# Softmax attention: a quarter of the denominator summed by ScalarE beside the maxima, the rest by GpSimd in three groups

## The reference, cut to what matters

```python
xn = layer_norm(x, norm_w, norm_b)
q = (xn @ q_w + q_b).reshape(Bx, Tx, H, -1)
k = (xn @ k_w + k_b).reshape(Bx, Tx, H, -1)
att = jnp.einsum('bnhl,bmhl->bnmh', q, k)
att = att + (1.0 - mask) * -1000000.0
att = jax.nn.softmax(att, axis=2)
v = ((xn @ v_w + v_b) * src_mask[:, :, None]).reshape(Bx, Tx, H, -1)
y = jnp.einsum('bnmh,bmhl->bnhl', att, v).reshape(Bx, Tx, Dx)
```

## Time and profile before

| | before |
|---|---|
| median of 3 runs | 5798.27 us (5793.98 to 5799.08) |
| profiled execution: time, span | 5799.68 us, 5797.9 us |
| share of the span busy: PE, DVE, ACT, POOL | 91%, 71%, 49%, 57% |
| attention stage, first max matmul to last output | 2527.5 to 4354.4 us of the span |
| one head in the middle of it | 55.57 us |

### The profile page before, as it was taken

How to read it: one execution, slowest core, us unless ns; L and a number is a source line. 1 busy time by engine, 2 the same in 40 slices (tenths; PEclk the granted TensorE clock), 3 DMA queues, 4 the chain that set the end, 5 groups by cost and what they waited for, 6 DMA issues and landing times. The chain is left out here.

```text
span 5797.9 us, 58781 instructions
## 1 busy us (share of the span) xinstructions
PE 5261.4 (91%) x19584; PEld 2493.5 (43%) x19584; DVE 4122.4 (71%) x5430; ACT 2814.3 (49%) x4847; POOL 3282.8 (57%) x2136
## 2 busy tenths in 40 slices
PE   7888988888898869989999999999998889979998
PEld 2333333333333324444554554555444454544545
DVE  6999999999999963267777777777744445444454
ACT  3757566675756523326666666666661131312112
POOL 3879797887979741128888888888890000000000
PEclk9999999999999999979999999999998999989999
DMA  4021211212122023321111111111103201021101
GB/s 167 22 102 60 86 73 51 79 46 102 37 100 83 29 104 123 124 62 34 23 34 30 27 34 23 34 33 24 34 1 134 82 26 69 17 104 35 60 26 51
DMA packets 117503, 346.28 MB, mean 60 GB/s; under 512 B 13040, under 2 KB 14288, under 8 KB 102800
## 3 DMA queue, kind: packets, MB, share of 16 engines
q1 hardware_dynamic: 99280, 294.47, 15.4%
q0 software_dynamic: 9216, 33.56, 1.5%
q10 hardware_dynamic: 8704, 14.50, 0.7%
HBM read 274.29 MB, written 67.67 MB: 59 GB/s over the span
## 5 line engine op out<-in xcount | busy, mean ns | idle before, releaser
L1397 DVE TENSOR_REDUCE attn_mx<-attn_ps_max 128x1 f32<-128x512 f32 x2048 | 1270.3, 683 | 404.1 <-PE attn_ps_max L1268 399.6
L425 POOL TENSOR_TENSOR mamba_hc<-mamba_h,mamba_bc 128x1024 f32<-128x1024 f32 x512 | 1219.1, 2381 | 360.0 <-DVE mamba_h L658 306.4
L1363 ACT ACTIVATE attn_prob<-attn_ps_s 128x512 f32<-128x512 f32 x2048 | 1061.0, 603 | 589.9 <-PE attn_ps_s L1293 586.6
L805 PE MATMUL mamba_y<-mamba_hc,ident 128*128 128x512 f32 x2048 | 997.7, 610 | 272.2 <-POOL mamba_hc L425 269.9
L1251 POOL TENSOR_TENSOR attn_pair_sum<-attn_prob 128x1024 f32<-128x1024 f32 x384 | 907.6, 2386 | 311.0 <-ACT attn_prob L1363 310.9
L528 ACT ACTIVATE mamba_da<-mamba_dt,mamba_a_neg 128x512 f32<-128x512 f32 x1024 | 691.0, 689 | 722.0 <-DVE mamba_h L658 718.3
L658 DVE TENSOR_TENSOR_SCAN mamba_h<-mamba_da,mamba_state,mamba_h 128x512 f32<-128x512 f32 x768 | 939.8, 1265 | 1.9 <-ACT mamba_da L528 1.9
L1293 PE MATMUL attn_ps_s<-attn_q_stack,attn_k_stack 100*128 100x512 f32 x2048 | 861.6, 424 | 4.2 <-ACT attn_prob L1363 4.2
L1268 PE MATMUL attn_ps_max<-attn_k_stack,attn_q_stack 98*128 98x512 f32 x2048 | 835.7, 415 | 16.8 <-DMA attn_q_stack<-qk_parts 16.0
L805 PEld LDWEIGHTS mamba_y<-mamba_hc,ident 128*128 128x128 f32 x2048 | 366.3, 191 | 856.5 <-POOL mamba_hc L425 459.2
L648 DVE TENSOR_TENSOR mamba_h<-mamba_du,mamba_bc 128x1024 f32<-128x1024 f32 x512 | 619.3, 1210 | 65.5 <-POOL mamba_state L427 57.1
(11 more groups left out here) (232 smaller groups left out, 6076.5 us busy)
## 6 DMA issues: line engine op xcount, KB each, us to landing
mamba_bc<-bc_dram SPq DMA_DIRECT2D x64, 1024.0 KB, 7.3
mamba_w<-in_in_proj_w_T SPq DMA_DIRECT2D x16, 2048.0 KB, 7.8
qk_parts<-qkv_pair POOLq DMA_DIRECT2D x64, 512.0 KB
attn_k_stack<-qk_parts SPq DMA_DIRECT2D x96, 256.0 KB
attn_q_stack<-qk_parts SPq DMA_DIRECT2D x96, 256.0 KB
mamba_x_in<-in_x SPq DMA_DIRECT2D x16, 1024.0 KB, 5.3
mamba_w<-in_out_proj_w_T SPq DMA_DIRECT2D x8, 2048.0 KB, 8.3
lin_norm_x<-x_after_L SPq DMA_DIRECT2D x16, 1024.0 KB, 5.7
```

The source lines that it names most:

```text
L425: nc.gpsimd.tensor_tensor(hc[:, gs % HC_SLOTS, :, :], h[:, gs % H_SLOTS, :, :], bc[:, g, G:2 * G, :], ALU.mult).then_inc(s["hc_done"], 1)
L805: mm = nc.tensor.matmul(y[ct % 2][:, :], ident[:, :], hc[:, gs % HC_SLOTS, j, :], start=(g == 0 and j == 0), stop=(g == NG - 1 and j == G ...
L1363: nc.scalar.activation(prob[kt % SLOTS][:, c * CH:(c + 1) * CH], ps_s[n % BANKS][:, :], ACT.Exp).then_inc(s["exp_done"], 1)
L1397: nc.vector.tensor_reduce(mx[hd % 3][:, qt, kc:kc + 1], ps_max[seq % BANKS][:, :], AX.X, ALU.max).then_inc(s["bank_read"], 1)
```

## The change

Every fourth key tile (`u % 4 == 3`, 3, 7, 11 and 15) leaves GpSimd's sums. The key block of a max matmul is no longer 512 neighbouring keys but four runs of 128 with a step of 512, so that the fourth block of a query tile holds the keys of just these four tiles. VectorE's reduce writes the negated maximum of this block, and ScalarE reads the block's scores from the same bank with this as bias, takes the exponentials and lets the engine accumulate them along the row (`sum_own`, 16 per head, into `own_sum`). The difference between the block's own maximum and the query's maximum is made by VectorE, its exponential by ScalarE (`exp_gap`), and the product is the block's share of the denominator (`scale_own`). `read_o` adds it before the reciprocal. GpSimd sums the other twelve tiles in three groups of four (0, 1, 2, 4; 5, 6, 8, 9; 10, 12, 13, 14): 18 adds, three waves of ones. `TURN_O` and `DEN_LAG` go from 2 to 3.

```diff
-        SIZES = (2, 3, 3, 2, 3, 3)
-        GROUPS = [tuple(range(sum(SIZES[:g]), sum(SIZES[:g + 1]))) for g in range(len(SIZES))]
-        NGRP = len(GROUPS)
+        OWN = QB - 1
+        SUMMED = [u for u in range(QT) if u % QB != OWN]
+        NGRP = 3
+        GROUPS = [tuple(SUMMED[g * len(SUMMED) // NGRP:(g + 1) * len(SUMMED) // NGRP]) for g in range(NGRP)]
...
-        TURN_O = 2
-        DEN_LAG = 2
+        TURN_O = 3
+        DEN_LAG = 3
...
             def free_bank(seq):
                 if seq >= BANKS:
                     pe.wait_ge(s["bank_read"], seq - BANKS + 1)
+                    if SEQ_OWN[seq - BANKS]:
+                        pe.wait_ge(s["own_summed"], OWN_BY[seq - BANKS + 1])
                 return ps_max[seq % BANKS]
...
-                nc.tensor.matmul(free_bank(seq)[:, :], q_st[slot][0:ROWS_MAX, qt * P:(qt + 1) * P],
-                                 k_st[slot][0:ROWS_MAX, kc * CH:(kc + 1) * CH], start=True, stop=True).then_inc(s["bank_filled"], 1)
+                nc.tensor.matmul(free_bank(seq)[:, :].rearrange("p (a j) -> p a j", j=P), q_st[slot][0:ROWS_MAX, qt * P:(qt + 1) * P],
+                                 k_st[slot][0:ROWS_MAX, :].rearrange("r (a b j) -> r b a j", b=QB, j=P)[:, kc],
+                                 start=True, stop=True).then_inc(s["bank_filled"], 1)
...
+            def sum_own(seq, hd, i):
+
+                act.wait_ge(s["bank_read"], seq + 1)
+                nc.scalar.activation(own_exp[:, :], ps_max[seq % BANKS][:, :], ACT.Exp, bias=mx[hd % 3][:, i // QB, OWN:QB],
+                                     accum_out=own_sum[hd % 3][:, i // QB:i // QB + 1]).then_inc(s["own_summed"], 1)
+
+            def exp_gap(hd):
+                act.wait_ge(s["gap_made"], hd + 1)
+                nc.scalar.activation(own_gap[:, :], own_gap[:, :], ACT.Exp, scale=-1.0).then_inc(s["gap_exp"], 1)
+
+            for i in range(OWN, NMAX, QB):
+                sum_own(i, 0, i)
             first_part(NMAX, 0)
+            exp_gap(0)
+            for i in range(OWN, LEAD * PER, QB):
+                sum_own(NMAX + 1 + i, 1, i)
...
                         elif hd + 1 < HEADS:
                             exp(hd + 1, 0, c)
+                    for j, tile in enumerate(max_tiles(hd, u)):
+                        if own_block(tile[1]):
+                            sum_own(item_at(hd, "max", u, j), *tile)
                     if u == TURN_O - 1 and hd:
                         copy_den(hd - 1)
                     if u == TURN_MAX and hd + 1 < HEADS:
                         first_part(item_at(hd, "turn_max", u), hd + 1)
+                        exp_gap(hd + 1)
                 copy_o(hd)
...
-                nc.vector.tensor_reduce(mx[hd % 3][:, qt, kc:kc + 1], ps_max[seq % BANKS][:, :], AX.X, ALU.max).then_inc(s["bank_read"], 1)
+                nc.vector.tensor_reduce(mx[hd % 3][:, qt, kc:kc + 1], ps_max[seq % BANKS][:, :], AX.X, ALU.max,
+                                        negate=own_block(i)).then_inc(s["bank_read"], 1)
                 if i == NMAX - 1:
                     dve.wait_ge(s["bank_read"], seq + 1)
-                    nc.vector.tensor_reduce(m_all[:, :], mx[hd % 3][:, :, :], AX.X, ALU.max).then_inc(s["m_done"], 1)
+                    nc.vector.tensor_reduce(m_all[:, :], mx[hd % 3][:, :, 0:OWN], AX.X, ALU.max).then_inc(s["m_others"], 1)
+                    dve.wait_ge(s["m_others"], hd + 1)
+                    nc.vector.scalar_tensor_tensor(out=m_all[:, :], in0=mx[hd % 3][:, :, OWN], scalar=-1.0, in1=m_all[:, :],
+                                                   op0=ALU.mult, op1=ALU.max).then_inc(s["m_done"], 1)
+                    dve.wait_ge(s["m_done"], hd + 1)
+                    nc.vector.tensor_tensor(own_gap[:, :], mx[hd % 3][:, :, OWN], m_all[:, :], ALU.add).then_inc(s["gap_made"], 1)
+
+            def scale_own(hd):
+                dve.wait_ge(s["gap_exp"], hd + 1)
+                dve.wait_ge(s["own_summed"], (hd + 1) * QT)
+                nc.vector.tensor_tensor(own_den[hd % 2][:, :], own_sum[hd % 3][:, :], own_gap[:, :], ALU.mult).then_inc(s["own_scaled"], 1)
...
-                nc.vector.reciprocal(rden[:, :].rearrange("p (t c) -> p t c", c=QB),
-                                     ps_d[:, :].rearrange("p (t c e) -> p t c e", c=QB, e=DH1)[:, :, :, 0]).then_inc(s["den_inv"], 1)
+                dve.wait_ge(s["own_scaled"], hd + 1)
+                nc.vector.tensor_tensor(rden[:, :].rearrange("p (t c) -> p t c", c=QB),
+                                        ps_d[:, :].rearrange("p (t c e) -> p t c e", c=QB, e=DH1)[:, :, :, 0],
+                                        own_den[hd % 2][:, :].rearrange("p (c t) -> p t c", c=QB), ALU.add).then_inc(s["den_whole"], 1)
+                dve.wait_ge(s["den_whole"], hd + 1)
+                dve.sem_inc(s["den_read"], 1)
+                nc.vector.reciprocal(rden[:, :], rden[:, :]).then_inc(s["den_inv"], 1)
```

More of the change, by code:

```diff
@@ L1157, in stage_attention @@
         m_all = r.sb("m_all", [P, QT])
+        own_exp = r.sb("own_exp", [P, CH])
+        own_sum = [r.sb(f"own_sum{i}", [P, QT]) for i in range(3)]
+        own_gap = r.sb("own_gap", [P, QT])
+        own_den = [r.sb(f"own_den{i}", [P, QT]) for i in range(2)]
         m_parts = r.sb("m_parts", [QT, 2, P], F32R)
@@ L1168, in stage_attention @@
         names = ("ones_set rows_set max_in bank_filled bank_read m_done m_first m_second s_mm exp_done "
-                 "o_mm o_copied sum_done den_mm den_copied den_turned den_inv den_read v_copied")
+                 "o_mm o_copied sum_done den_mm den_copied den_turned den_inv den_read v_copied "
+                 "m_others gap_made gap_exp own_summed own_scaled den_whole")
         s = {n: r.sem(n) for n in names.split()}
@@ L1189, in bank_items, with own_block @@
             return items
+        def own_block(i):
+            return i % QB == OWN
         BEFORE = NMAX + 1 + LEAD * PER
@@ L1198, in item_at @@
             return first_item[hd] + bank_items(hd).index((kind, u, j))
+        SEQ_OWN = [own_block(i) for i in range(NMAX)] + [False] + [own_block(i) for i in range(LEAD * PER)]
+        for hd in range(HEADS):
+            SEQ_OWN += [kind == "max" and own_block(max_tiles(hd, u)[j][1]) for kind, u, j in bank_items(hd)]
+        OWN_BY = [0]
+        for own_here in SEQ_OWN:
+            OWN_BY.append(OWN_BY[-1] + own_here)
         @block.sync
@@ L1249, in _ @@
                                 pool.wait_ge(s["sum_done"], hd * ADDS + used[units[n], half])
-                            first = pair_sum[g % 2] if n else prob[units[0] % SLOTS]
-                            nc.gpsimd.tensor_tensor(pair_sum[g % 2][:, at], first[:, at], prob[unit % SLOTS][:, at],
+                            first = pair_sum[(hd * NGRP + g) % 2] if n else prob[units[0] % SLOTS]
+                            nc.gpsimd.tensor_tensor(pair_sum[(hd * NGRP + g) % 2][:, at], first[:, at], prob[unit % SLOTS][:, at],
                                                     ALU.add).then_inc(s["sum_done"], 1)
@@ L1314, in den_mm @@
                     mm = nc.tensor.matmul(ps_d[c * DH1:(c + 1) * DH1, :], ones[:, :],
-                                          pair_sum[g % 2][:, c * CH:(c + 1) * CH], start=(g == 0), stop=(g == NGRP - 1))
+                                          pair_sum[(hd * NGRP + g) % 2][:, c * CH:(c + 1) * CH], start=(g == 0), stop=(g == NGRP - 1))
                 mm.then_inc(s["den_mm"], 1)
@@ L1361, in exp @@
                     before, unit = divmod(hd * QT + kt - SLOTS, QT)
-                    act.wait_ge(s["sum_done"], before * ADDS + used[unit, c // 2])
+                    if (unit, c // 2) in used:
+                        act.wait_ge(s["sum_done"], before * ADDS + used[unit, c // 2])
                 nc.scalar.activation(prob[kt % SLOTS][:, c * CH:(c + 1) * CH], ps_s[n % BANKS][:, :], ACT.Exp).then_inc(s["exp_done"], 1)
@@ L1429, in _ @@
             second_part(NMAX, 0)
+            scale_own(0)
             for i in range(LEAD * PER):
@@ L1439, in _ @@
                         second_part(item_at(hd, "turn_max", u), hd + 1)
+                        scale_own(hd + 1)
             read_o(first_item[HEADS], HEADS - 1)
```

1 line of the change is left out of this document (removed).

## The result

| | before | after |
|---|---|---|
| median of 4 runs each, side by side | 5798.31 us | 6001.41 us (5985.9 to 6012.56) |
| ratio to before | | 1.035 [1.0326, 1.0374] |
| span of the profiled execution | 5797.9 us | 6002.0 us |
| ahead of head 0's first combined maximum | 2566.7 us | 2576.1 us |
| from there to head 31's | 1723.2 us | 1925.0 us |

What follows compares the result with a forecast made beforehand. TensorE was taken to bound the attention stage, except in head 31. 5799.7 - 81 (waves) + 94 (stalls) + 12 (start) - 5 (end) = 5819.7, stated as 5818 us; range 5766 to 5865.

Steps and rivals of the forecast that it cites:

- the price of the small VectorE operations: Per head: scaling the own sum takes 0.2 us; three operations on the maxima at `u` = 12 cost nothing.
- The dearest with a time of its own: Rival: own sums hold ScalarE 0.88 instead of 0.69 us, about 1.8 us more per head, 5873 us; chance 0.06.
- the wide end of the strided keys: Rival: strided max matmuls slow, 0.34 instead of 0.24 us between two, 215 us in all; chance 0.04.
- The late ScalarE: Heads: own sum delays the next unit's exponentials, the fourth score load is 0.29 us late, a plain unit loses 0.16.
- the ledger: List of added stalls per head, by unit: 3.09 us against a gain of 2.61, 94 us for some 30.5 heads.
- `read_o`'s 0.26: Unit 4: the add over PSUM before the reciprocal lengthens the output read, 0.26 us per head.
- The waves: Heads 0 to 30: three fewer waves of ones per head at 0.87 us each, saving 81 us.
- The end: Head 31: TensorE waits for GpSimd, whose adds fall from 20 to 18, saving 5 us.
- The start: Head 0's 64 maxima: bank refills wait for own sums, 9 us; 12 us with the following terms.
- the 1.5 and 1.2 on top of it: After head 0's maxima: three own tiles ahead of head 1 add 1.5 us, first exponentials queueing behind the third 1.2.
- The clock: Attention stage: TensorE has its full granted clock; no term for losing it.
- the half case: Rival: half the lateness or less, ScalarE sooner or TensorE's queue absorbing more; 5769 us with half; chance 0.22.

Runs made afterwards that it cites:

- the contiguous keys: Changed kernel with gap add and own-share multiply as one-SBUF-input reduces, max tiles reading 512 neighbouring keys: 5825.81 us, ratio 1.0051 to the kernel before.
- the kernel with one-input operations: Changed kernel with gap add and own-share multiply replaced by one-SBUF-input reduces, gap and scaling left out of the computation: 5821.08 us, ratio 1.0057 to the kernel before.
- the early one: Changed kernel, gap and scaling on GpSimd, own block second, maxima combined by one min reduce, waves three units behind: 5740.61 us, ratio 0.9903 to before.
- the last version shown above: Changed kernel, gap and scaling on GpSimd, own block second, maxima combined by one min reduce, waves five units behind: 5730.34 us, ratio 0.9884 to before.

## Why the prediction was wrong, point by point

- **The step that failed** is the price of the small VectorE operations: `scale_own` at 0.2, and "The three small VectorE operations for the maxima at `u` = 12: the wave of ones in that unit covers them, and without it they would cost 0.15 per head." One of those three (`own_gap`'s add) and `scale_own`'s product take 2.2 and 2.9 us on average, and cost 6 us per head instead of nothing: 1925.0 - 1739.0 (the version with both on GpSimd) = 186 us over 31 heads. I had priced them by the small operations of the profile before, and every one of these has at most one input in SBUF beside PSUM, or is a reduce. I asked how long VectorE works on them, and not which other engine was at work. None of my rivals had this. The dearest with a time of its own ended at 5873; the wide end of the strided keys, 215 us, would have reached as far, but the contiguous keys rule it out.
- **Where the rule stood.** The Trainium skill, "SBUF — State Buffer", section "Who interferes with whom", says that a VectorE instruction with two SBUF inputs contends with a GpSimd instruction that reads SBUF, and one with at most one such input, outside the modes that use two ports, doesn't. The traces here agree: 2.28 against 0.19 us at one place of the kernel before. It would have named both operations from the diff, and the combination of the maxima. What the rows add is that the wait isn't bounded by one GpSimd instruction: 4.29, 6.87 and 9.19 us across a row of them, in which the adds start 2.34 us apart.
- **The late ScalarE** was sized about right, and its mechanism holds. The own sum takes 0.688 us (0.69 predicted) and starts 0.23 after the next unit does, so a plain unit loses 0.16. The timeline of the kernel after:

```profile
3303.64 0.50 PE L1313 MATMUL attn_ps_s<-attn_q_stack,attn_k_stack 100*128 100x512 f32 x1
...
3303.87 0.69 ACT L1399 ACTIVATE attn_own_exp<-attn_ps_max,attn_mx 128x512 f32<-128x512 f32 x1 [0.69 <-DVE attn_mx L1437]
...
3305.19 0.19 PEld L1313 LDWEIGHTS attn_ps_s<-attn_q_stack,attn_k_stack 100*128 100x128 f32 x1 [0.24 <-ACT attn_prob L1384]
...
3306.86 0.50 PE L1313 MATMUL attn_ps_s<-attn_q_stack,attn_k_stack 100*128 100x512 f32 x1
...
3309.92 0.50 PE L1313 MATMUL attn_ps_s<-attn_q_stack,attn_k_stack 100*128 100x512 f32 x1
```

  The units are 3.22 and 3.06 long, the loss and the recovery of the ledger, against 3.05 in the earlier trace rows. This load sits idle 0.24 us (lateness 0.29 in the ledger), and those behind `copy_den` and `copy_o` 0.72 each (0.80 and 0.61, the second too small). Term by term, in the kernel with one-input operations, against units that nothing delays (3.06 us, and 3.20 for unit 14; medians over 28 heads): units 7, 9 and 11 lose 0.42 together (0.48 in the ledger), unit 3 0.63 (0.67), unit 5 0.27 (0.27), unit 14 0.74 (0.74), unit 15 0.27 (0.19), unit 0 0.38 (0.48). As a whole, with the same waves and the same turn: 55.9 us per head with the late own sum and 53.4 with the early one, 2.5 apart, and 53.2 with the waves five units behind; the ledger had 3.09 less `read_o`'s 0.26, 2.83.
- **The waves** gave what they should: 0.87 us each, 2.61 per head. **The end** gave 5.5 to 7.1 (5). **The start** cost 6.9 to 9.4 up to the first combined maximum, where I had 9; the 1.5 and 1.2 on top of it were too dear: from the first combination to the second it takes 56.0 us, and 56.2 in the kernel before. **The strided keys** cost nothing that the runs can tell, as said.
- **The clock.** I had TensorE at full clock throughout. It is in the head of the last version shown above (1.00). In the kernel after it fell to 0.50 behind the standstill of 3.1 us, and the unit behind took 1.1 to 2.2 us longer than with one-input operations, a part of the 6 above.
- **The chances.** "Slower" had 0.53 for a reason that holds (the version on GpSimd is 0.4% slower), but it came true mostly for another: about 20 of the 203 us are the terms that I had listed, and that part alone is what the prediction earned. The range of 5766 to 5865 had no term for what one engine does to another. It also didn't follow from its own parts: the half case is 5769 and the dear end of the own sum 5873.

## What to carry to other kernels

Before pricing a small VectorE operation by its size, count its inputs in SBUF and look at what GpSimd does at that moment: with two inputs beside a row of GpSimd adds, 0.2 us became 2 to 9. The remedy is to write it with one SBUF input (a reduce over neighbouring columns, signs chosen so that one `min` does, or an input left in PSUM), or to give it to GpSimd itself. An operation of this kind that is short in a trace may only have started in the last moment before a border between two GpSimd adds, so a change elsewhere can make it long. And once it is gone, a sum that reads the same PSUM bank as a reduce is worth placing early: here the order on ScalarE was worth 2.5 us per head.

## What the runs showed of the hardware that was not expected

- In a row of GpSimd adds, a VectorE operation with two SBUF inputs that starts 0.05 to 0.08 us before the border between two adds takes 0.18 (185 of 186). One that starts 0.01 us before it, as the added one in the kernel before does, takes 2.40, the whole next add. From 0.12 behind it on it takes 2.27 (to the next border) or the rest of the row: 6.87 where 6.96 are left, 9.19 where 9.29 are.
- With one input in PSUM and one in SBUF the same operation isn't held. `read_o`'s add over the denominators lies wholly inside a GpSimd add in 31 of 32 heads and took 177 ns on average, in the groups by line of the kernel after:

```profile
L1466 DVE TENSOR_TENSOR attn_rden<-attn_ps_d,attn_own_den 128x16 f32<-128x16 f32 x32 | 5.7, 177 | 92.4 <-PE attn_ps_d L1303 92.4
```

- GpSimd does the 128x16 add in 0.24 us and the product in 0.22, hardly slower than VectorE undisturbed (0.18); the version with them on GpSimd took 5821.64 us, the one with one-input operations on VectorE 5821.08.
- While VectorE waits, GpSimd isn't slowed: its adds take 2381 ns on average in the kernel after and 2387 in the kernel before. The 61 adds of the kernel after that have a held VectorE operation beside them for over 2 us take 2370, the others 2383.
